# A dynamic-filter convolution stage on one Trainium2 core: splitting the final sum over two adding stores, moving small moments to ScalarE, and giving TensorE a second product to add

## The reference

```python
# x: (16, 512, 64, 64)
x = x + conv4x4(_gn(x), kernel)                 # layer 0: group norm, one 4x4 filter for all channels
x = x + L1(_gn(x), w_v, w1, gamma, beta, w2, b2)  # layer 1

# L1(x):
t   = relu(group_norm(d4_1x1(x, w1), gamma, beta, cmid))      # 32 groups of 8 channels
wgt = einsum('oi,bighw->boghw', w2, t) + b2                   # 9 weights per pixel, group and g
xv  = d4_1x1(x, w_v)                                          # values
pats = unfold_patches(xv, 3)                                  # 3x3 neighbourhood, 9 taps
out = (wv * pats).sum(axis=4)                                 # wv: wgt, taps turned per g
```

## Time and profile before

| | |
|---|---|
| median of 3 runs | 5064.24 us |
| profiled execution | 5067.52 us, span of its profile 5065.8 us |
| TensorE busy | 4251.4 us (84%) |
| VectorE busy | 4474.8 us (88%) |
| ScalarE busy | 2860.6 us (56%) |
| GpSimd busy | 4133.2 us (82%) |
| granted TensorE clock, mean | 0.941 of 2.4 GHz |
| stage B from the first rstd (L1027) to the last | 1209.0 to 4807.9 us, 15 periods |

### The profile page before, as it was taken

How to read it: one execution, slowest core, us unless ns; L and a number is a source line. 1 busy time by engine, 2 the same in 40 slices (tenths; PEclk the granted TensorE clock), 3 DMA queues, 4 the chain that set the end, 5 groups by cost and what they waited for, 6 DMA issues and landing times.

```text
span 5065.8 us, 115951 instructions
## 1 busy us (share of the span) xinstructions
PE 4251.4 (84%) x38012; PEld 1455.9 (29%) x38012; DVE 4474.8 (88%) x7761; ACT 2860.6 (56%) x4642; POOL 4133.2 (82%) x2208
## 2 busy tenths in 40 slices
...
GB/s 237 256 258 256 258 256 258 256 133 88 126 94 117 93 117 101 105 103 104 113 97 113 97 122 93 113 103 116 94 125 93 116 92 116 97 113 101 96 75 65
DMA packets 872958, 679.47 MB, mean 134 GB/s; under 512 B 560224, under 2 KB 822752, under 8 KB 856032
## 3 DMA queue, kind: packets, MB, share of 16 engines
...
q0 software_dynamic: 36864, 134.23, 17.2%
...
## 4 chain that ended last, share of the span: by engine, by line
POOL 44%; issue 13%; DVE 11%; PE 8%; POOLq 1%; ACT 1%; DVEq 0%; DMA 0%; SPq 0%; ACTq 0%
POOL acc L1046 43%; DVE prod_d L1098 3%; DVE prod_p L1098 2%; PE ps L783 2%; PE ps L770 2%; DVE ps L1142 2%; PE ps L793 1%; PE ps L742 1%; DVE ps L1098 1%; PE ps L732 1%; DVE six_t L1063 1%; DVE acc L1146 1%; POOL out L1035 1%; DVE x_bias L1090 1%; POOLq L1043 0%
## 5 line engine op out<-in xcount | busy, mean ns | idle before, releaser
L1046 POOL TENSOR_TENSOR acc<-acc,prod_p 128x1024 f32<-128x1024 f32 x1280 | 3093.1, 2417 | 302.9 <-DVE acc L1146 155.9
L1098 DVE TENSOR_TENSOR prod_p<-ps,val 128x1024 f32<-128x1024 f32 x1280 | 1558.6, 1218 | 128.8 <-POOL acc L1046 121.1
L793 PE MATMUL ps<-prod_d,base 128*128 128x512 f32 x1024 | 633.5, 703 | 583.8 <-DVE prod_d L1098 572.7
L1098 DVE TENSOR_TENSOR prod_d<-ps,val 128x512 f32<-128x512 f32 x1536 | 1041.5, 681 | 2.4 <-ACT ps L947 2.4
L300 PE MATMUL ps<-xn,band 64*64 64x512 f32 x8192 | 948.2, 598 | 21.5 <-issue 13.0
L742 PE MATMUL ps<-xh,wh 128*32 128x512 f32 x6144 | 765.8, 630 | 33.3 <-ACT t L906 21.9
L332 POOL TENSOR_TENSOR x_out<-x_out,x_in 128x512 f32<-128x512 f32 x512 | 636.4, 1275 | 0.0
L260 ACT ACTIVATE x_out<-ps 64x512 f32<-64x512 f32 x1024 | 606.3, 592 | 50.6 <-PE ps L300 29.2
L941 ACT ACTIVATE val<-ps 128x512 f32<-128x512 f32 (+1 forms) x640 | 356.3, 557 | 461.4 <-PE ps L770 453.8
L783 PE MATMUL ps<-t,w 128*32 128x256 f32 x9216 | 574.4, 401 | 40.2 <-DVE prod_d L1098 35.1
L770 PE MATMUL ps<-xm,base 128*32 128x256 f32 (+1 forms) x8192 | 589.3, 425 | 15.9 <-ACT xm L921 15.7
...
## 6 DMA issues: line engine op xcount, KB each, us to landing
x_in<-x SPq DMA_DIRECT2D x128, 1024.0 KB, 7.4
x<-x_out SPq DMA_DIRECT2D x256, 512.0 KB, 5.1
xr<-x SPq DMA_DIRECT2D x512, 256.0 KB, 3.5
out<-x SPq DMA_DIRECT2D x1024, 128.0 KB, 2.7
out<-acc POOLq DMA_DIRECT2D x256, 512.0 KB, 5.6
...
```

The source lines that it names most:

```text
L793: nc.tensor.matmul(ps[:, D_BANK, :], same, prod_d[:, 0, :], start=False, stop=True, skip_group_check=True)\
L1046: nc.gpsimd.tensor_tensor(acc[:, r, :], acc[:, r, :], prod_p[:, k % P_RING, :], ALU.add).then_inc(p_added, 1)
L1098: return nc.vector.tensor_tensor(dst.rearrange("p (m r w) -> p m r w", m=count, w=W), taps_of(tap).rearrange("p (m r w) -> p m r w", m=1, ...
```

## The change

1. GpSimd sums only its own products: the first whole product (tap 4) is written by VectorE straight into a new buffer `sum_p` (two of them), and GpSimd adds four instead of five. It no longer adds to `acc`, so it no longer waits for `acc` before its adds.
2. Each granule is stored by two adding stores: `acc` (`store_own`, after GpSimd's add of product 2) and `sum_p` (`store_sum`, of the granule before, after the add of product 1, and after its `acc` store has landed). `acc` has two buffers instead of four; the copy of x1 still runs at most four granules ahead, and now waits for the second store.
3. In half 1 of a granule TensorE adds products 1 and 2 into the bank, and VectorE's sum L1142 is made in half 0 only.
4. The small operations on the moments of t go from VectorE to ScalarE (`keep_means`, `keep_variances`, `t_affine`), and the two small matmuls take banks of the ring of two. The power on GpSimd stands after its add of product 1 in granule 14 instead of after the last add of granule 13. The scale and offset are made right before relu of the next image.

```diff
-ACC_RING = 4
+ACC_RING, SUM_RING, COPY_RING = 2, 2, 4
+NADD = NP - 1
+OWN_AT, SUM_AT = 2, 1
-RSTD_AT = (13, 4)
+RSTD_AT = (14, 1)
...
         def add_one(i, n, half):
-            pe.wait_ge(own, i * (OWN * N_GRAN) + OWN * n + OWN // 2 * half + 2)
-            nc.tensor.matmul(ps[:, D_BANK, :], same, prod_d[:, 0, :], start=False, stop=True, skip_group_check=True)\
-                .then_inc(pe_added, 1)
+            g = i * (OWN * N_GRAN) + OWN * n + OWN_A * half
+            pe.wait_ge(own, g + 2)
+            mm = nc.tensor.matmul(ps[:, D_BANK, :], same, prod_d[:, 0, :], start=False, stop=(half == 0),
+                                  skip_group_check=True)
+            if half == 1:
+                pe.wait_ge(own, g + 3)
+                mm = nc.tensor.matmul(ps[:, D_BANK, :], same, prod_d[:, 1, :], start=False, stop=True,
+                                      skip_group_check=True)
+            mm.then_inc(pe_added, 1)
...
+        def keep_means(i):
+            b = take()
+            nc.scalar.activation(minus_mean, ps[:, b, 0:MT], ACT.Copy, scale=-1.0).then_inc(kept, 1)
+            act.wait_ge(kept, chunk_end(i, "means", 0))
+            for m in range(MT):
+                last = nc.scalar.activation(dev[:, m:m + 1], mv[:, m, 0:1], ACT.Identity, bias=minus_mean[:, m:m + 1])
+            last.then_inc(t_moments, 1)
+            act.wait_ge(t_moments, 3 * i + 1)
+            for m in range(MT):
+                last = nc.scalar.activation(spread[:, m:m + 1], dev[:, m:m + 1], ACT.Identity,
+                                            bias=mv[:, m, 1:2], scale=dev[:, m:m + 1])
+            last.then_inc(t_spread, 1)
...
         def relu(i, u):
-            act.wait_ge(t_norm, i + 1)
+            if u == 0:
+                t_affine(i)
...
+        def store_own(i, n):
+            r, c = n % ACC_RING, n % COPY_RING
+            pool.wait_ge(own, i * (OWN * N_GRAN) + OWN * (n + 1))
+            wait_apart(pool, pool_apart, copied[c], i * (64 * N_GRAN // COPY_RING) + 64 * (n // COPY_RING + 1))
+            nc.gpsimd.dma_start(out[i, n], acc[:, r, :], accum_op=ALU.add).then_inc(own_stored[r], 16)
+        def store_sum(i, n):
+            img, at = (i, n) if n >= 0 else (i - 1, n + N_GRAN)
+            r = at % SUM_RING
+            pool.wait_ge(p_added, i * (NADD * N_GRAN) + NADD * (n + 1))
+            wait_apart(pool, pool_apart, own_stored[at % ACC_RING], i * (16 * N_GRAN // ACC_RING) + 16 * (n // ACC_RING + 1))
+            nc.gpsimd.dma_start(out[img, at], sum_p[:, r, :], accum_op=ALU.add).then_inc(sum_stored[r], 16)
         def period(i, more=True):
             for n in range(N_GRAN):
-                r = n % ACC_RING
-                pool.wait_ge(own, i * (OWN * N_GRAN) + OWN * (n + 1))
-                for j in range(NP):
...
-                    nc.gpsimd.tensor_tensor(acc[:, r, :], acc[:, r, :], prod_p[:, k % P_RING, :], ALU.add).then_inc(p_added, 1)
+                total = sum_p[:, n % SUM_RING, :]
+                for j in range(1, NP):
...
+                    nc.gpsimd.tensor_tensor(total, total, prod_p[:, k % P_RING, :], ALU.add).then_inc(p_added, 1)
+                    if j == SUM_AT and not first(i, n):
+                        store_sum(i, n - 1)
+                    if j == OWN_AT:
+                        store_own(i, n)
                     if more and (n, j) == RSTD_AT:
                         t_rstd_of(i + 1)
-                store(i, n)
...
         def pooled(i, n, j):
...
+            if j == 0:
+                dst = sum_p[:, n % SUM_RING, :]
+                if not first(i, n - SUM_RING + 1):
+                    dve.wait_ge(sum_stored[n % SUM_RING], i * (16 * N_GRAN // SUM_RING) + 16 * (n // SUM_RING))
...
             product(n, 3, prod_d[:, 2, :], m0, QM // 2).then_inc(own, 1)
-            dve.wait_ge(own, g + 3)
             dve.wait_ge(pe_added, i * (2 * N_GRAN) + 2 * n + a + 1)
-            nc.vector.tensor_tensor(ps[:, D_BANK, :], ps[:, D_BANK, :], prod_d[:, 1, :], ALU.add).then_inc(own, 1)
-            dve.wait_ge(own, g + 5)
+            if a == 0:
+                dve.wait_ge(own, g + 3)
+                nc.vector.tensor_tensor(ps[:, D_BANK, :], ps[:, D_BANK, :], prod_d[:, 1, :], ALU.add).then_inc(own, 1)
+            dve.wait_ge(own, g + (5, 4)[a])
             if a == 0 and not first(i, n - ACC_RING + 1):
-                dve.wait_ge(stored[r], i * (16 * N_GRAN // ACC_RING) + 16 * (n // ACC_RING))
+                dve.wait_ge(own_stored[r], i * (16 * N_GRAN // ACC_RING) + 16 * (n // ACC_RING))
```

More of the change, by code:

```diff
@@ L476, in stage_b @@
     acc = sb("acc", [P, ACC_RING, QM * UPX])
+    sum_p = sb("sum_p", [P, SUM_RING, QM * UPX])
     prod_p = sb("prod_p", [P, P_RING, QM * UPX])
@@ L493, in stage_b @@
     rstd = x1_bias[:, 6:6 + MT]
+    minus_mean = x1_bias[:, 16:16 + MT]
+    eps = x1_bias[:, 18:19]
     t_scale = x1_bias[:, 8:8 + MT]
@@ L556, in order_of_period @@
             if more:
+                if n == MOMENTS_AT:
+                    yield ("means", 0), 1
                 yield from order_of_half(n, BLOCK_T_1, INVERSE_1, BLOCK_V_1, FORWARD_1)
+                if n == MOMENTS_AT:
+                    yield ("variances", 0), 1
                 yield from order_of_half(n, BLOCK_T_2, INVERSE_2, BLOCK_V_2, FORWARD_2)
@@ L656, in copy_resid @@
         def copy_resid(i, n):
-            u, q4, r = (n // GRANS) % UNITS, n % GRANS, n % ACC_RING
-            if not first(i, n - ACC_RING + 1):
-                wait_apart(sp, sp_apart, stored[r], i * (16 * N_GRAN // ACC_RING) + 16 * (n // ACC_RING))
+            u, q4, r = (n // GRANS) % UNITS, n % GRANS, n % COPY_RING
+            if not first(i, n - COPY_RING + 1):
+                wait_apart(sp, sp_apart, sum_stored[r % SUM_RING],
+                           i * (16 * N_GRAN // SUM_RING) + 16 * ((n - COPY_RING) // SUM_RING + 1))
             img, at = i + n // N_GRAN, n % N_GRAN
@@ L695, in _ @@
         period(B - 1, more=False, ahead=False)
+        for r in range(COPY_RING):
+            sp.wait_ge(copied[r], 64 * B * N_GRAN // COPY_RING)
         for r in range(ACC_RING):
-            sp.wait_ge(resid_in[r], 64 * B * N_GRAN // ACC_RING)
-            sp.wait_ge(stored[r], 16 * B * N_GRAN // ACC_RING)
+            sp.wait_ge(own_stored[r], 16 * B * N_GRAN // ACC_RING)
+        for r in range(SUM_RING):
+            sp.wait_ge(sum_stored[r], 16 * B * N_GRAN // SUM_RING)
     @block.tensor
@@ L818, in _ @@
         pe.wait_ge(w2_built, 1)
+        means(0)
+        variances(0)
         pe.wait_ge(xm_edges, EDGES)
         values(0)
-        means(0)
-        variances(0)
         tap_weights(0, 0, EARLY + LATE)
@@ L912, in keep_inverse, with keep_variances, t_affine @@
                 nc.scalar.activation(t_chunk(m, c), ps[:, b, :], ACT.Copy).then_inc(kept, 1)
+        def keep_means(i):
+            b = take()
+            nc.scalar.activation(minus_mean, ps[:, b, 0:MT], ACT.Copy, scale=-1.0).then_inc(kept, 1)
[8 more added lines that the diff above has]
+            last.then_inc(t_spread, 1)
+        def keep_variances(i):
+            b = take()
+            nc.scalar.activation(var_eps, ps[:, b, 0:MT], ACT.Identity, bias=eps).then_inc(kept, 1)
+        def t_affine(i):
+            act.wait_ge(t_rstd, i + 1)
+            for m in range(MT):
+                last = nc.scalar.activation(t_scale[:, m:m + 1], rstd[:, m:m + 1], ACT.Identity, scale=gam[:, m:m + 1])
+            last.then_inc(t_moments, 1)
+            act.wait_ge(t_moments, 3 * i + 2)
+            for m in range(MT):
+                last = nc.scalar.activation(t_bias[:, m:m + 1], minus_mean[:, m:m + 1], ACT.Identity,
+                                            bias=bet[:, m:m + 1], scale=t_scale[:, m:m + 1])
+            last.then_inc(t_moments, 1)
+            act.wait_ge(t_moments, 3 * i + 3)
         def edges(i):
```

92 lines of the change are left out of this document (34 added, 58 removed).

## The result

| kernel | median us | runs | ratio to before, 95% interval |
|---|---|---|---|
| before | 5063.1 | 4 (5059.03 to 5066.26) | |
| changed | 4991.85 | 4 (4987.63 to 4995.38) | 0.9859 [0.9842, 0.9876] |

The change saves 1.4%. The prediction was 4879 us (3.65% less): the sign is right and the time is inside the range, but 185 us were forecast and 71 came.

The account below looks back on a forecast made before the run. GpSimd bound most granules before; TensorE was to become the bound: 222.4 + 6 - 3.5 + 3.5 = 228.4, say 229 us a period. 15 x (239.9 - 229) = 163.5, plus 20 and 2, is 185.5 off: 4879 us, range 4750 to 5010.

Parts of the forecast that it names:

- near 95%: Sign expected in the changed kernel's profile: TensorE's busy share of a period.
- named as the sign: Expected in the profile: a period of 225 to 234 us between two rows of GpSimd's power, L1089.
- The ring of the second store: VectorE's whole product waits for the `sum_p` store to land: 12.0 to 12.4 us around, under a 14 us granule, priced at nothing.
- binds mildly: Rival: with `sum_p` store landings of 7.5 us, 14.3 us a granule and 236 a period, 4990 us; chance 0.23.
- ScalarE's small operations: Ten more small operations on ScalarE, 1.5 to 4.5 us, taken as 4; mostly hidden, as ScalarE is busy 115.7 of 240.
- The hand-over rival: Between images, ScalarE's small operations and bank order delay relu and taps by 10 us a period: about 5060; chance 0.04.
- The bound is not reached freely: TensorE is made to wait at its adds where VectorE is late, in light granules and granules 13 to 15.
- 6 + 3.5 = 9.5 us a period: TensorE's waits: 6 in granules 13 to 15, 3.5 in light granules with extra statistics or half 0 waiting for an add.
- TensorE after: TensorE's 239.9 - 34.5 = 205.4 us a period plus 17.0 for 16 more adds makes 222.4, so TensorE becomes the bound.
- up to 0.7 us in light granules only: Cost in half 1 of product 2 ending about 1.7 us after product 1, with a whole product between them.
- no slack to give: Granule 10 on TensorE runs 13.34 us without a wait, 14.4 with the third add; held against VectorE setting the pace.
- the clock rule: Activity lifts TensorE's throttled clock: alone 5 us a period more than the 3.5 taken, and a sum 75 us lower.

Follow-up runs that it names:

- experiment 5: The changed kernel with the loops over images 1 to 14 written out on VectorE, TensorE, ScalarE and GpSimd: 4916.57 us, 0.9719.
- experiment 2: The kernel before with the middle periods of TensorE and VectorE written out instead of looped: 5016.33 us, 0.9912.
- Experiment 4: The changed kernel, but in half 1 VectorE makes product 2 right behind product 1, ahead of the whole product: 4895.63 us, 0.9671.
- experiment 6: The changed kernel with product 2 of half 1 made right behind product 1 and all four engines' loops written out: 4861.66 us, 0.9606.
- experiment 3: The changed kernel without part 3: VectorE makes its sum in both halves, TensorE adds product 1 only: 4899.34 us, 0.9675.
- experiment 7: The kernel before with part 3 alone: TensorE adds products 1 and 2 in half 1, VectorE's sum there goes: 5097.32 us, 1.0079.
- experiment 1: The changed kernel with the middle periods of TensorE and VectorE only written out instead of looped: 4975.62 us, 0.9835.
- experiment 8: The kernel before with part 4 alone: small moments on ScalarE, the power behind GpSimd's second add of granule 14: 4981.46 us, 0.9847.

## Why the prediction was wrong

**What was right.** GpSimd is no bound after: its line left the chain, its wait ahead of the power went, and TensorE leads the chain as the forecast said. But it leads by 36% to VectorE's 24%, its share of a period is 88% (208.4 of 235.5) where "near 95%" was forecast, and the period lies above the 225 to 234 that were named as the sign: neither engine is the bound alone. The ring of the second store doesn't bind: VectorE waited for the store of `sum_p` 8 times in 1300 to 4700 us, 4.3 us in all, and the landings' medians are 5.5 and 6.1 us against 5.6 before. The time is that of the rival "binds mildly" (4990) by chance only: its mechanism did not take place, and this rival is refuted. (The ring's terms add up to 11.9 to 12.2 us, not 12.0 to 12.4; nothing hangs on it.) ScalarE's small operations take 0.17 to 0.38 us each, ten of them 2.9 us, against 4 taken. The hand-over rival asked for 10 us a period lost and is refuted: the chain of moments gained.

**The step that failed: "The bound is not reached freely".** It sized TensorE's waits at its adds as 6 + 3.5 = 9.5 us a period. They are 21.8 in the period shown, 12.3 more (19.6 in the mean of 15 periods, 10.1 more). Of the 21.8, 4.5 are the turn, 4.8 the wait for product 2, and 12.5 the waits for product 1 that the forecast put at 9.5. (Of that, the 6 in granules 13 to 15 is 6.4 by its own terms: 42.6 less 36.5 + 3.2 - 3.5.) The rest of TensorE's period came out 5.2 shorter than forecast, 235.5 - 21.8 = 213.7 instead of 222.4 - 3.5 = 218.9. Together that is the 7.1 us between 228.4 and 235.5; against the rounded 229 of the sum it is 6.5, over 15 periods 98 us of the miss of 113. Two terms were missing or too small:

- *The turn of the loop, not in the sum at all.* It costs 5.8 us at each of 13 turns (experiment 5). The trace before had it, in two disguises (rows of the kernel before, at the turn):

```profile
3140.52 1.23 DVE L1098 TENSOR_TENSOR prod_p<-ps,val 128x1024 f32<-128x1024 f32 x1 [3.20 <-POOL acc L1046]
3144.27 1.20 PE L793 MATMUL ps<-prod_d,base 128*128 128x512 f32 x2 [2.46 <-DVE prod_d L1098]
```

  VectorE's gap at the turn (2.8 to 4.0 us) carried GpSimd's add as its releaser at 12 of 13 turns. TensorE's wait for the late product was part of the 34.5 us of the earlier trace rows, which the step "TensorE after" subtracted, putting only 9.5 back. Granule 0 of the table shows it: 18.03 before, 13.78 in experiment 2.
- *Product 2 as a deadline.* The prediction saw that product 2 ends 1.7 us after product 1 and priced it at "up to 0.7 us in light granules only", with no term of its own in the sum. Experiment 4 prices it at 96 us in the medians, and at 5.1 us a period in the traces. The 0.6 us that TensorE waits was seen rightly (L814). What was left out is that VectorE stands behind the same add: its last sum now waits for product 2's matmul, and its idle at the sums is 4.8 us a period larger than with product 2 first. How that lateness passes on to later granules was not followed.

Both together are worth 130 us (experiment 6), more than the miss of 113 us; each alone brings the period near 230 us (230.4 and 230.2), so they overlap. Without both it is 227.4 us, 1.0 below the forecast 228.4.

**The gain that didn't exist.** Behind both terms is a sum that was not made: the change without part 3. By the forecast's own terms VectorE would be its bound, at 208.8 + 16 x 0.73 + 4 x 1.7 = 227.3 us a period, less than the 228.4 with part 3. So its own numbers gave part 3 no gain. As written, part 3 costs 93 us (experiment 3), and 40 in the kernel before (experiment 7). The forecast's 229 us a period is what experiment 3 measured for the kernel without part 3 (229.3), but that is luck: the two are sums of different terms, and the forecast has no turn in it. Of the 10.6 us a period that parts 1, 2 and 4 gain together (239.9 to 229.3), part 3 gives 6.2 back, and 4.4 are left.

**Smaller terms.** Behind the last power it is 13 us instead of 20, ahead of the first nothing instead of 2. Granule 10 on TensorE, from first add to first add, takes 14.1 us (a row at 3016.71 and one at 3030.82), 14.4 was forecast. In experiment 4 the same stretch takes 14.11 in each of twelve periods (from 3212.34 to 3226.45, for one), so "no slack to give" was right for granule 10 on TensorE. The 12.72 of the table is not that stretch: it runs from one row of VectorE's to the next. VectorE's granules 10 and 11 are 12.7 and 15.0 there.

**The clock.** TensorE's busy time for the old work and the 17.0 us of adds would be 198.1 + 17.0 = 215.1 us; 208.4 is measured, 6.7 less, with the granted clock at 0.97 in the period instead of 0.94. As an estimate, 215.1 x 0.94 / 0.97 = 208.4. At the hand-over the 96 tap matmuls take 5.99 us, 7.22 before. The prediction took 3.5 off for it. The trace lies between this and the 8.5 that the prediction drew from the clock rule, nearer to the latter. That rule is the Trainium skill's, "TensorE: Matmul & The Clock Gate", section "Part 1: The HAM clock gate" (throttled by default, lifted by activity); the trace agrees with its direction, 0.94 to 0.97 with more work. The time won did not shorten the period as forecast, since the waits grew by more.

## What to carry to other kernels

Work moved to another engine has to be priced with its deadlines: if engine A's next instruction waits for B's new one, A and B wait in turn, and neither looks full though both set the pace. Then try the order before the amount: two instructions exchanged gave 96 us here, as much as the part's whole cost. Idle time at an instruction is not slack until its cause is known: 16 us a period of extra work, for a TensorE that idled 24 us a period at its adds (experiment 3: 362.8 us in 15), cost 10.3. And a gap at the top of a loop body that changes its releaser from period to period may be the loop's own: write the loop out, on every engine, to see.

## What was new about the chip

- A hardware loop's turn costs time on each engine: in the changed kernel's 13 turns VectorE is idle 2.4 to 3.1 us and TensorE 2.75 to 5.3, and in experiment 1 ScalarE up to 4.25 and then up to 2.2 more. At 13 turns it costs the changed kernel 5.8 us each and the kernel with product 2 first 2.6 each ((4895.63 - 4861.66) / 13). Written out, the instructions cost nothing that the times show: each of the six kernels so changed got faster.
- GpSimd spends 868 ns on issuing the adding store of `sum_p` and 1157 ns on that of `acc` in the same period. Before it was 0.88 us, with 0.64 us idle ahead of it. Why the two differ was not tried.
- GpSimd's power takes 1.0 us right behind a store's issue and 0.7 us between two adds: the first two rows are of the changed kernel, the third is of experiment 8.

```profile
3087.25 0.86 POOL L1106 DMA_DIRECT2D out<-sum_p  x1
3087.86 0.99 POOL L1089 TENSOR_TENSOR x_bias<-x_bias,power_b 128x2 f32<-128x2 f32 x1
```
```profile
3087.92 0.71 POOL L1078 TENSOR_TENSOR x_bias<-x_bias,power_b 128x2 f32<-128x2 f32 x1
```
